# Releasing the next batch's gather at the start of the output projection instead of inside the feed-forward stage

## The chip, the cores and the metric

The kernel runs on one core of one Trainium2 chip. The metric is the device time of one execution in microseconds (us), the median of several runs. The names of the engines are those of the profile: PE is TensorE (PEld its weight loads), DVE is VectorE, ACT is ScalarE, POOL is GpSimd, SP is SyncE. A name with a q (DVEq, POOLq) is the sequencer of that engine, which handles waits and semaphore instructions.

## The reference

Two transformer-like layers over `x` of 4 batches x 1024 tokens x 256 features, float32, each sublayer followed by a residual and a layer norm:

```python
x = ln(x + L0_attn(x))   # a linear state recurrence (scan over the sequence), then a projection
x = ln(x + L0_ffn(x))    # mixture of 8 experts, top 2, each 256 -> 512 -> 256
x = ln(x + L1_attn(x))   # pre-norm softmax attention, 16 heads of 16, projection; it adds its own residual
x = ln(x + L1_ffn(x))    # gated SiLU, 256 -> 704 -> 256, activations and weights quantised to FP4 blocks of 16
```

In the mixture, each token's result is the weighted sum of two experts' results: `out = s0 * y[expert 0] + s1 * y[expert 1]`.

## The kernel before, in words

The kernel has two parts. The first works on all four batches: the scan, the first layer norm, the routing, and then 39 tiles of 256 tokens each through the experts. The expert results are stored in device memory in `y_slot`, in the order of the tiles, and the layer's input is kept in `x_mid`.

The second part is a loop over the four batches, written once and run by every engine as a hardware loop (`Fori(0, B)`). One turn of the loop does, for one batch of 1024 tokens (8 tiles of 128):

1. **Gather (POOL, L457 to L467).** POOL waits for the semaphore flow `qsf`. It then loads the batch's part of `x_mid` (1 MB) into `Xin`, copies the row numbers into `posb` (L461), and issues 16 indirect DMAs (L466), one for each of 8 tiles and each of the two chosen experts, from `y_slot` into `Y1` and `Y2` (128 rows of 1 KB each). `Y1` lies in `Qh`, `Y2` in `Kh`, and `Xin` in the upper half of `V`.
2. **Combine and norm (DVE, L1173 to L1185).** DVE waits for the gather's semaphores, forms `R = Xin + s0*Y1 + s1*Y2` (L1179, L1182), and computes two layer norms.
3. **Attention.** PE turns the tokens, computes Q, K and V, and then for each of 8 head pairs the scores twice (L786 for the row maxima that DVE takes at L1203, L816 for the exponentials that ACT takes at L592) and the weighting of V (L829). POOL sends the maxima as rows (L477), 4 DMAs for each pair.
4. **Output projection.** PE turns the heads' results back (`heads_turn`, L859, flow `op`). DVE divides them by the sums (L1243, L1246). PE turns them again (L881), ACT copies (L601), PE projects (L870, L871), and DVE adds twice the residual (`proj_add`, L1230). This is repeated for 8 tiles.
5. **Norm and quantise (DVE).** The third layer norm (`layer_norm(2, ...)`, L1153 to L1170) and two halves of the FP4 quantiser (L1103 to L1113).
6. **Feed-forward, 8 tiles.** For tile `t`: PE computes gate and up (L903), ACT takes SiLU (L617), DVE multiplies (L1268, flow `hh`) and quantises (L1103 to L1113, flow `hq`), PE turns (L930), ACT copies, PE computes down (L913), and DVE adds the residual (`ffn_add`, L1235).
7. **Last norm and store.** DVE writes `X`, SP stores it.

`qsf` tells POOL that the buffers of the gather are free. Its semaphore is incremented once ahead of the loop (L1139), which releases the gather of the first batch. Inside the loop DVE increments it once in each turn, in the kernel before in tile `t == 1` of the feed-forward stage (L1271, L1272). That increment releases the gather of the next batch; the one of the last turn releases nothing. POOL's queue is in order: it comes to this wait after the last DMA of L477 of the current batch.

All DVE operations that depend on one another are joined by waits on a semaphore (`link`, L1144). An engine's instructions run in the order in which they are written.

Of the kernel before, what the change touches and what calls it, by code (L numbers as in the profile page):

```python
# [78 lines left out]
def transformer(nc, xT, state_cols, WtT, WbT, Wc4, WoT, Dv, bo, sel, Wg, W1, b1, W2, b2, rev,  # L79
                lnw_d, lnb_d, Wqkv, bqkv_d, Wproj, bproj, w_gate, w_up, w_down, ident_d, out):  # L80
    ctx = ExitStack()
    with ctx:
# [853 lines left out]
        def _(dve):  # L936
# [204 lines left out]
            with dve.Fori(0, B) as b:  # L1141
# [91 lines left out]
                def ffn_add(t):  # L1233
                    F["dp"].wait(dve, b, t + 1)
                    F["dr"].inc(dve.tensor_tensor(R2[:, t, :], PS[:, 6 + t % 2, 0:D], X[:, t, :], ALU.add))  # L1235

                for n in range(TT):
                    i, qh = n // 2, n % 2
                    F["op"].wait(dve, b, i + 1)
                    heads = PS[:, 2 * (i % 2):2 * (i % 2) + 2, :].rearrange("p k (h q c) -> p (k h) q c", q=2, c=32)  # L1240
                    if n:
                        F["on"].wait(dve, b, n)
                    link(dve.reciprocal(rc[:, qh, :], heads[:, :, qh, DH]))  # L1243
                    if n >= 2:
                        F["mp"].wait(dve, b, n - 1)
                    F["on"].inc(dve.tensor_tensor(ON[n % 2].rearrange("p (h d) -> p h d", d=DH), heads[:, :, qh, 0:DH],  # L1246
                                                  rc[:, qh, :].unsqueeze(2).to_broadcast([P, HEADS, DH]), ALU.mult))
                    if n >= 2:
                        proj_add(n - 2)
# [16 lines left out]
                for t in range(TT):  # L1266
                    F["sg"].wait(dve, b, t + 1)
                    F["hh"].inc(dve.tensor_tensor(Hb.rearrange("p (a n) -> p a n", a=2), PS[:, 2:4, 0:IH],  # L1268
                                                  SGb.rearrange("p (a n) -> p a n", a=2), ALU.mult))
                    F["hh"].wait(dve, b, t + 1)  # L1270
                    if t == 1:  # L1271
                        dve.sem_inc(F["qsf"].sem, 1)  # L1272
                        F["qsf"].seen += 1
                    for q, ins in enumerate(quant(Hb, P, I, HQ, qn_h, qm_h)):
                        if q < 9:
                            link(ins)
                            if q == 8 and t:
                                F["htp"].wait(dve, b, t)
                        else:
                            F["hq"].inc(ins)  # L1280
                    if t:
                        ffn_add(t - 1)
# [56 lines left out]
```

How the kernel before makes its waits and increments, by code:

```python
    def wait(self, eng, b, n):  # L61
        eng.wait_ge(self.sem, b * self.per + n)
# [12 lines left out]
    def wait(self, eng, n):  # L75
        eng.wait_ge(self.sem, n)
# [240 lines left out]
        @block.sync  # L317
# [75 lines left out]
            load_ffn(1, w_up)  # L393
            load_ffn(2, w_down)
            for k in range(TILES):
                if k + 2 < TILES:
                    load_x(k + 2)
                if k + 1 < TILES:
                    e_next = load_w1(k + 1)
                load_w2(k, e_now)
                e_now = e_next
            sp.wait_ge(s_wev, len(turns))
            sp.wait_ge(s_one, 1)
            for k in range(NB):
                for a in range(2):
# [14 lines left out]
                            for dst, src in ((Qs, qp), (Ks, kp)):  # L421
                                at = ROW * a + row * DH
                                F[f"stk{k}"].inc(sp.dma_start(dst[at:at + DH, k, :].bitcast(F32), src), by=16)
                F["xn"].wait(sp, b, 4 * TT)
                hold(sp, "sp")
                F["outd"].inc(sp.dma_start(out.rearrange("(n p) d -> p n d", p=P)[:, bass.ds(b * TT, TT), :],
                                           X[:, :, :]), by=16)
                F["outd"].wait(sp, b, 16)
                sp.sem_inc(F["xfree"].sem, 1)
                F["xfree"].seen += 1
            sp.wait_ge(F["outd"].sem, 16 * B)
# [51 lines left out]
        @block.scalar  # L483
        def _(act):
            act.preload_act_table_set("natural_log_exp_and_others")
            act.wait_ge(s_const, N_CONST)
            act.wait_ge(s_proT, 2)
            act.wait_ge(s_pro, 2)
```

## Time and profile before

| what | value |
|---|---|
| median of 3 runs | 2095.88 us |
| the 3 runs | 2093.76, 2095.88, 2103.21 us |
| the profiled execution's own time | 2103.21 us |
| its span, first to last instruction | 2101.5 us |
| mean granted TensorE clock over the span | 0.861 of full speed |
| busy share of the span | PE 79%, PEld 45%, DVE 63%, ACT 37%, POOL 11% |

The profile is of one execution. Between the span and the execution's own time lie 1.7 us. Busy shares are means over stages that have different limits, so they don't say what one edit is worth; that is read from the waits and the timeline around it. In a row of waits, the columns are the waiting engine and line, what ended the wait, the total in us, how often, and the longest. In a row of the timeline they are the start in us from the span's start, the duration in us (of all of a merged group), the engine, line, operation, what is written and read, and in square brackets the engine's idle time ahead of it and what ended it.

### The profile page before, as it was taken

Reading aid. Unit: us, or ns where it says so; the run is one execution under the profiler, and the core shown is the slowest. Engines: PE = TensorE matmul, PEld = TensorE weight load, DVE = VectorE, ACT = ScalarE, POOL = GpSimd, SP = SyncE. Lnnn points to the kernel's source line nnn. Section 1 sums busy time; section 2 is a strip of 40 time slices with the busy share of each in tenths; the row PEclk is TensorE's granted clock in tenths of the full one; section 3 lists DMA queues with packets and bytes.
Section 4 is the critical chain, followed back from the end, with each engine's and each line's share of the span. In section 5 each row is a group of like instructions: output and inputs, shape, how many; then the busy total and the mean of one; then the engine's idle time right before and its main releaser. Section 6 shows DMA issues by size and latency. Waiting matters only on the chain.

```text
span 2101.5 us, 26524 instructions
## 1 busy us (share of the span) xinstructions
PE 1656.3 (79%) x7920; PEld 945.7 (45%) x7920; DVE 1333.0 (63%) x2678; ACT 782.2 (37%) x1145; POOL 229.0 (11%) x308
## 2 busy tenths in 40 slices
PE   5751899997389996938999877499996938999686
PEld 2651788886143333624333345243334624333354
DVE  3324223210589956877899287788846877898386
ACT  0220223322127772212676511137671111676421
POOL 0235000002201000300100030000000300001000
PEclk8865899999579997967899988679997967899898
DMA  3223777775131100203120010122000103110000
GB/s 123 73 93 114 247 233 228 228 230 167 34 59 32 32 2 1 61 22 60 18 46 2 1 53 9 42 43 44 17 2 0 61 22 61 29 35 2 1 1 20
DMA packets 90965, 133.77 MB, mean 64 GB/s; under 512 B 17002, under 2 KB 65516, under 8 KB 90812
## 3 DMA queue, kind: packets, MB, share of 16 engines
q1 hardware_dynamic: 76364, 100.15, 18.2%
q0 software_dynamic: 14448, 31.74, 4.5%
q8 instruction: 77, 1.26, 0.3%
q14 instruction: 76, 0.62, 0.1%
HBM read 76.71 MB, written 29.36 MB: 50 GB/s over the span
## 4 chain that ended last, share of the span: by engine, by line
PE 59%; DVE 22%; issue 8%; DMA 3%; ACT 3%; SPq 3%; POOL 1%; another core or an unknown queue 0%; DVEq 0%; ACTq 0%; POOLq 0%
PE PS L786 10%; PE PS L829 10%; DVE MX L1203 9%; PE PS L903 7%; PE PS L710 6%; PE PS L722 6%; PE PS L913 4%; PE PS L816 2%; DVE st L1153 2%; PE PS L764 2%; PE PS L660 2%; PE PS L772 2%; PE PS L870 1%; DVE X L1170 1%; ACT Pb L592 1%
## 5 line engine op out<-in xcount | busy, mean ns | idle before, releaser
L1203 DVE TENSOR_REDUCE MX<-PS 128x1 f32<-128x512 f32 x1024 | 636.4, 682 | 83.5 <-PE PS L786 83.1
L592 ACT ACTIVATE Pb<-PS 128x1024 f32<-128x1024 f32 x512 | 497.8, 1023 | 231.5 <-PE PS L816 230.9
L786 PE MATMUL PS<-Ks,Qs 48*128 48x512 f32 x1024 | 390.6, 494 | 46.5 <-DMA Ks<-OT 19.2
L786 PEld LDWEIGHTS PS<-Ks,Qs 48*128 48x128 f32 x1024 | 175.2, 203 | 365.0 <-DVE MX L1203 326.0
L816 PE MATMUL PS<-Qs,Ks 50*128 50x512 f32 x1024 | 309.7, 453 | 11.8 <-DMA Qs<-MR 5.9
L829 PE MATMUL PS<-Pb,V 128*32 128x512 f32 x2048 | 283.5, 627 | 2.8 <-ACT Pb L592 2.8
L816 PEld LDWEIGHTS PS<-Qs,Ks 50*128 50x128 f32 x1024 | 147.5, 195 | 65.9 <-ACT Pb L592 53.2
L477 POOL DMA_DIRECT2D Qs<-MR x128 | 65.4, 518 | 1024.9 <-DVE MR L1216 597.6
L1135 DVE TENSOR_TENSOR V<-PS,V 128x512 f32<-128x512 f32 x39 | 27.0, 692 | 217.6 <-PE PS L722 217.6
L722 PE MATMUL PS<-Pb,OT 128*128 128x256 f32 x624 | 141.0, 379 | 0.0
L538 ACT ACTIVATE OT<-PS,V 128x256 f32<-128x256 f32 x156 | 65.4, 470 | 159.8 <-PE PS L710 159.8
L753 PE MATMUL PS<-ident,OT 128*128 128x128 f32 x64 | 17.8, 448 | 134.1 <-DVE OT L1170 134.1
L722 PEld LDWEIGHTS PS<-Pb,OT 128*128 128x128 f32 x624 | 115.7, 190 | 14.2
L913 PE MATMUL PS<-wdT,Pb 128*128 128x256 f32 (+1 forms) x384 | 102.5, 412 | 8.0 <-ACT Pb L629 8.0
L903 PE MATMUL PS<-wgT,XT 128*128 128x352 f32 x256 | 92.7, 509 | 16.9 <-DVE OT L1268 8.7
L913 PEld LDWEIGHTS PS<-wdT,Pb 128*128 128x128 f32 (+1 forms) x384 | 74.5, 202 | 35.2 <-issue 10.9
L903 PE MATMUL PS<-wuT,XT 128*128 128x352 f32 x256 | 81.7, 462 | 0.0
L617 ACT ACTIVATE OT<-PS 128x704 f32<-128x704 f32 x32 | 24.2, 757 | 152.7 <-PE PS L903 152.7
L1243 DVE RECIPROCAL rc<-PS 128x16 f32<-128x16 f32 x32 | 8.1, 253 | 107.4 <-PE PS L859 106.6
L710 PE MATMUL PS<-OT,Pb 128*128 128x256 f32 x320 | 75.6, 391 | 0.7 <-ACT OT L529 0.7
L753 PEld LDWEIGHTS PS<-ident,OT 128*128 128x128 f32 x64 | 12.2, 206 | 139.6 <-DVE OT L1170 135.7
L829 PEld LDWEIGHTS PS<-Pb,V 128*32 128x32 f32 x2048 | 40.8, 109 | 74.9 <-issue 65.5
(233 smaller groups left out, 2007.4 us busy)
## 6 DMA issues: line engine op xcount, KB each, us to landing
Pb<-W SPq DMA_DIRECT2D x78, 512.0 KB, 3.9
OT<-x_slot SPq DMA_DIRECT2D x39, 256.0 KB, 4.0
y_slot<-V POOLq DMA_DIRECT2D x39, 256.0 KB, 4.2
Qs<-Qh SPq DMA_DIRECT2D x128, 64.0 KB, 2.3
Ks<-Kh SPq DMA_DIRECT2D x128, 64.0 KB, 2.4
V<-b SPq DMA_DIRECT2D x39, 128.0 KB, 4.3
V<-x_mid POOLq DMA_DIRECT2D x4, 1024.0 KB
out<-X SPq DMA_DIRECT2D x4, 1024.0 KB, 4.6
```

What stands on the lines that cost most here:

```text
L477: F["mrow"].inc(pool.dma_start(Qs[r:r + 1, p % NB, :].rearrange("o (t q) -> o t q", t=TT).bitcast(F32), MR[at:at + TT, p % 2, :].bitcast(F ...
L538: C["hr"].inc(act.activation(HTm[k % 2][:, hc, :], PS[:, 2 + 2 * (k % 2) + hc // 2, hc % 2 * ST:(hc % 2 + 1) * ST], ACT.Relu, bias=b1t[:, ...
L592: F["ex"].inc(act.activation(Pb[:, kt % 2, 2 * qh:2 * qh + 2, :], PS[:, 2 * qh:2 * qh + 2, :], ACT.Exp, scale=0.25))
L660: pe.matmul(o, xTb[b][:, c, t * P:(t + 1) * P], Gm[:, c, :], start=(c == 0), stop=False)
L710: ins = pe.matmul(PS[:, 2 + 2 * (k % 2) + hc // 2, hc % 2 * ST:(hc % 2 + 1) * ST], W1t[k % 2][:, c, hc * P:(hc + 1) * P], XTm[k % 2][:, c, :],
L722: ins = pe.matmul(PS[:, 6 + k % 2, a * D:(a + 1) * D], HTm[k % 2][:, hc, a * P:(a + 1) * P], W2t[k % 2][:, hc, :], start=(hc == 0), stop=( ...
L786: F["slp"].inc(pe.matmul(PS[:, slot_bank(i), :], Qs[rows, p % NB, t * P:(t + 1) * P], Ks[rows, p % NB, kh * HALF:(kh + 1) * HALF], start=T ...
L816: ins = pe.matmul(PS[:, 2 * qh + a, :], Ks[rows, p % NB, kt * P:(kt + 1) * P], Qs[rows, p % NB, qh * HALF:(qh + 1) * HALF], start=True, st ...
L829: ins = pe.matmul(PS[32 * j:32 * j + 32, 7, :], V[:, kt, 2 * p + a, :], Pb[:, kt % 2, 2 * qh + a, :], start=(kt == 0), stop=(kt == KT - 1) ...
L903: ins = pe.matmul(PS[:, 2 * w + a, 0:IH], XT[:, c, t * P:(t + 1) * P], wT[:, c, a * IH:(a + 1) * IH], start=(c == 0), stop=(c == DC - 1))
L913: ins = pe.matmul(PS[:, 6 + t % 2, 0:D], HT[0:k, c, :], wdT[0:k, c, :], start=(c == 0), stop=(c == IC - 1))
L1203: F["sld"].inc(dve.tensor_reduce(MX[:, p % 2, a, t, kh:kh + 1], PS[:, slot_bank(i), :], AX.X, ALU.max))
```

## The change

DVE's increment of `qsf` is taken out of tile 1 of the feed-forward stage and put ahead of the 8 tiles of the output projection. In front of it stands a wait for the first group of turned heads (`op`), the same wait that the first tile's reciprocal has anyway. Nothing else is changed: POOL's instructions and their order, the number of DMAs and their sizes, and the increment ahead of the loop are as before.

```diff
@@ -1234,6 +1234,9 @@
                     F["dp"].wait(dve, b, t + 1)
                     F["dr"].inc(dve.tensor_tensor(R2[:, t, :], PS[:, 6 + t % 2, 0:D], X[:, t, :], ALU.add))
 
+                F["op"].wait(dve, b, 1)
+                dve.sem_inc(F["qsf"].sem, 1)
+                F["qsf"].seen += 1
                 for n in range(TT):
                     i, qh = n // 2, n % 2
                     F["op"].wait(dve, b, i + 1)
@@ -1268,9 +1271,6 @@
                     F["hh"].inc(dve.tensor_tensor(Hb.rearrange("p (a n) -> p a n", a=2), PS[:, 2:4, 0:IH],
                                                   SGb.rearrange("p (a n) -> p a n", a=2), ALU.mult))
                     F["hh"].wait(dve, b, t + 1)
-                    if t == 1:
-                        dve.sem_inc(F["qsf"].sem, 1)
-                        F["qsf"].seen += 1
                     for q, ins in enumerate(quant(Hb, P, I, HQ, qn_h, qm_h)):
                         if q < 9:
                             link(ins)
```

## Rows read from the trace of the kernel before

**Rows 1.** The page, section 4: the chain that ended last, by engine.

```profile
PE 59%; DVE 22%; issue 8%; DMA 3%; ACT 3%; SPq 3%; POOL 1%; another core or an unknown queue 0%; DVEq 0%; ACTq 0%; POOLq 0%
```

**Rows 2.** The waits of all engines over the whole span.

```profile
POOL V L459 <- DVEq L1272: 239.1, 3, 80.2
...
DVE OT L1179 <- DMA Kh<-y_slot,posb: 24.5, 4, 12.2
```

**Rows 3.** The timeline around the first batch's gather, 515 to 560 us.

```profile
517.79 0.91 POOL L459 DMA_DIRECT2D V<-x_mid  x1 [2.68 <-DMA y_slot<-V]
...
526.40 0.88 DVE L1179 SCALAR_TENSOR_TENSOR OT<-Qh,svb,V 128x256 f32<-128x256 f32 x2 [12.22 <-DMA Kh<-y_slot,posb]
...
538.62 0.94 POOL L466 DMA_INDIRECT Kh<-y_slot,posb  x1 [0.30 <-issue]
...
541.36 0.88 DVE L1179 SCALAR_TENSOR_TENSOR OT<-Qh,svb,V 128x256 f32<-128x256 f32 x2 [4.04 <-DMA Kh<-y_slot,posb]
```

**Rows 4.** POOL's timeline, the second batch's gather, first and last instruction.

```profile
851.16 0.93 POOL L459 DMA_DIRECT2D V<-x_mid  x1 [80.19 <-DVEq L1272]
...
873.79 1.46 POOL L466 DMA_INDIRECT Kh<-y_slot,posb  x1 [0.30 <-issue]
```

**Rows 5.** DVE's timeline, where the second batch's combine begins.

```profile
928.10 3.26 DVE L1179 SCALAR_TENSOR_TENSOR OT<-Qh,svb,V 128x256 f32<-128x256 f32 x8 [0.23 <-DVE svb L1173]
```

**Rows 6.** DVE's timeline in feed-forward tiles 0 to 2, first and last loop turn.

```profile
842.87 0.89 DVE L1103 TENSOR_REDUCE qmx<-OT 128x44 f32<-128x704 f32 x1
...
849.41 0.88 DVE L1268 TENSOR_TENSOR OT<-PS,OT 128x704 f32<-128x704 f32 x1
850.45 0.89 DVE L1103 TENSOR_REDUCE qmx<-OT 128x44 f32<-128x704 f32 x1 [0.15 <-DVE OT L1268]
...
858.17 0.42 DVE L1235 TENSOR_TENSOR V<-PS,X 128x256 f32<-128x256 f32 x1 [0.67 <-PE PS L913]
858.51 0.88 DVE L1268 TENSOR_TENSOR OT<-PS,OT 128x704 f32<-128x704 f32 x1
...
2017.87 0.88 DVE L1268 TENSOR_TENSOR OT<-PS,OT 128x704 f32<-128x704 f32 x1
...
2026.98 0.88 DVE L1268 TENSOR_TENSOR OT<-PS,OT 128x704 f32<-128x704 f32 x1
```

**Rows 7.** Windows over tiles 1 to 3: DVE busy (instructions), PEclk, DMA share, GB/s.

```profile
850.40:875.55 25.15, 21.85 (x34) 1.00 0.40 121
...
2018.86:2043.80 24.94, 21.38 (x34) 1.00 0.00 1
```

**Rows 8.** The same two windows, of L1110 alone and of L1111 alone.

```profile
850.40:875.55 25.15, 1.87 (x3) 1.00 0.40 121
2018.86:2043.80 24.94, 1.58 (x3) 1.00 0.00 1
...
850.40:875.55 25.15, 2.67 (x3) 1.00 0.40 121
2018.86:2043.80 24.94, 2.67 (x3) 1.00 0.00 1
```

**Rows 9.** DVE's timeline in the output projection and the norm behind it, first loop turn.

```profile
795.55 0.26 DVE L1243 RECIPROCAL rc<-PS 128x16 f32<-128x16 f32 x1 [27.38 <-PE PS L859]
...
799.27 0.42 DVE L1230 SCALAR_TENSOR_TENSOR V<-X,PS 128x256 f32<-128x256 f32 x1 [1.37 <-PE PS L871]
...
813.85 0.42 DVE L1230 SCALAR_TENSOR_TENSOR V<-X,PS 128x256 f32<-128x256 f32 x1 [1.26 <-PE PS L871]
...
819.60 2.67 DVE L1170 TENSOR_SCALAR X<-V,mv,rstd 128x256 f32<-128x256 f32 x8
822.19 1.21 DVE L1103 TENSOR_REDUCE qmx<-X 128x64 f32<-128x1024 f32 x1
```

**Rows 10.** The chain that ended last in order of time: projection, and two turns' first gate and up.

```profile
797.58 1.03 PE PS L870 x4
...
813.19 0.64 PE PS L871 x2
...
1221.60 8.07 PE PS L903 x16
...
2003.20 6.40 PE PS L903 x16
```

## The prediction

> **What bounds the kernel now.** I read the views in this order. The page's chain by engine comes first: 59% of it is PE, 22% DVE, and 3% DMA [rows 1]. So only a small part of the end is set by transfers, and what I must know is whether the moved gather belongs to that part. The waits answer it. DVE waits for the gather 24.5 us in total, in 4 pieces, the longest 12.2 us [rows 2]. There are four loop turns, so these four pieces could be one in each turn. The timeline shows that they are not: the first is 12.22 us ahead of the combine at 526.40, the last is 4.04 us at 541.36, and the other two lie between them [rows 3]. All four belong to the first batch's gather, which starts at 517.79 right behind the mixture's last store. That gather is released by the increment ahead of the loop, which the change does not touch.
>
> The gathers that the change does move are those of batches 1, 2 and 3. POOL stands idle for them 239.1 us in 3 pieces, each about 80 us, waiting for DVE's increment [rows 2]. The second batch's starts at 851.16 and its last instruction ends at 873.79 + 1.46 = 875.25 [rows 4]. DVE reads its result first at 928.10, and what it waited for then was its own copy of the weights, for 0.23 us, and no transfer [rows 5]. So the gather is finished 928.10 - 875.25 = 52.9 us before it is used, less the landing of its last transfer. For that I take the first batch: the last issue ended at 538.62 + 0.94 = 539.56, and DVE could go on at 541.36 [rows 3], 1.8 us later. About 51 us of slack remain. The other two moved gathers look alike.
>
> **The change part by part.**
>
> (a) *The gather starts earlier.* In the first turn DVE is released by PE at 795.55 [rows 9], the new place of the increment. POOL would start some 0.8 us behind it, as it starts at 851.16 behind the increment that follows the multiply of 849.41 + 0.88 = 850.29 [rows 4, 6]. So it would start near 796.4, about 54.8 us earlier than now. POOL's 80.19 us of idle time [rows 4] show that it is free by 771, so the start really moves. Work hidden before is hidden now with some 106 us of slack instead of 51. Gain: 0. There is no wait there to shorten.
>
> (b) *The gather leaves the feed-forward stage.* Here the trace holds its own comparison. In the last turn there is no gather, and the same 34 DVE instructions of tiles 1 to 3 take 21.38 us busy; with a gather beside them they take 21.85 us [rows 7]. A gather thus stretches DVE's work by 0.47 us, of which L1110, a single-source operation in SBUF, has 1.87 - 1.58 = 0.29 us; L1111, with two SBUF inputs, is the same, 2.67 and 2.67 us [rows 8]. Does DVE's stretch reach the end? From the multiply of tile 1 to that of tile 2 it takes 858.51 - 849.41 = 9.10 us with a gather and 2026.98 - 2017.87 = 9.11 us without, and DVE still waits 0.67 us for PE in between [rows 6]. PE sets the pace and DVE's 0.47 us lies beside it. The removed increment costs 0.15 us of gap in tile 1 against 0.03 us at the same place in tile 0 (842.87 follows directly) [rows 6], also inside that wait. Gain: 0; if DVE were on the path it would be 0.47 + 0.12 = 0.6 us per gather, 3 x 0.6 = 1.8 us. I take 0.
>
> (c) *The gather comes beside the projection and the third norm.* POOL's part lasts from 851.16 to 875.25, 24.1 us, now [rows 4], and 539.56 - 517.79 = 21.8 us where DVE was mostly waiting [rows 3]. From 796.4 it would end between 818.2 and 820.5. Up to 813.85 the chain is PE's, L870 and L871 in turn [rows 10], and DVE waits for PE ahead of its additions, 1.37 us at 799.27 and 1.26 us at 813.85 [rows 9]. So stretches there are hidden. From 813.85 on the chain is DVE's norm. That leaves 820.5 - 813.9 = 6.6 us of overlap on the path. By the price of (b), 0.47 us in 24.1 us, this is 0.13 us. From below it is 0, because the single-source operations of the norm come at its end, from 819.60 on [rows 9], when POOL has nearly finished. From above it is all 0.47 us. I take 0.13 us, for 3 gathers 0.4 us. Nothing reaches the quantiser from 822.19 on, which has the kind of operation that was stretched.
>
> The rule that speaks against this move is in the Trainium skill, "GPSIMD Engine Reference", section "Key points": GpSimd shares its SBUF interfaces with VectorE, and they contend where a VectorE instruction runs in a 2-port mode or has two SBUF inputs. The trace agrees on L1110 and shows nothing on DVE's side for L1111, 2.67 us either way [rows 8]. The Trainium skill, "VectorE: DVE Perf Modes", section "Why PSUM operands drop a tier", says that an operand in PSUM excludes the 2-port mode, so the projection's DVE work, which all reads PSUM, would be exposed less; by that the sum would be 0.4 us smaller at most.
>
> (d) *The increment on DVE ahead of the first reciprocal.* It is on the chain: PE's turned heads release DVE at 795.55 [rows 9], and the increment stands between. Behind it in DVE's queue are all of the projection's operations, for which PE waits. The nearest row is the gap of (b), 0.15 - 0.03 = 0.12 us; from below it is 0, if the sequencer takes it within its own latency. The added wait is for the same value as the next one, and costs no more than that. I take 0.12 us in each of the 4 turns, 0.5 us.
>
> (e) *Other queues.* SP issues nothing between the attention's stacks and the last store, and POOL's next work behind the gather is the next batch's maxima, over 100 us later. ACT has no operation added. The DMA engines are 0.40 busy during a gather and 0.00 without one [rows 7], with PE at the same pace.
>
> Sum: 0 + 0 + 0.4 + 0.5 = +0.9 us. Against the profiled execution's 2103.21 us this gives 2104.1. That execution is the slowest of the three runs, and the change touches nothing that made it so; carried to the median of 2095.88 the sum gives 2096.8, which I round to **2097 us**.
>
> **The rivals.** A measurement of this kernel can tell about 0.5%, 10.5 us, from no change; that is 3.5 us for each of the three moved gathers.
>
> *Rival 1, slower: POOL's issuing stalls DVE and PE in the projection.* The projection passes each tile from PE to DVE to PE to ACT and back, and a stall in any link could add up. The largest single delay that I would price is the 0.29 us of L1110 over three tiles [rows 8], charged once to each of POOL's 17 DMA instructions: 17 x 0.29 = 4.9 us per gather, 14.8 us in all, with the increment 2111 us. It decides from 0.2 us per POOL instruction. Against it: the whole of 34 DVE instructions lost only 0.47 us beside a gather [rows 7], and PE's pace did not change.
>
> *Rival 2, faster: the feed-forward stage is relieved.* If DVE's stretch were on the path, 1.8 us come back, and 2094 us results, still no measurable change. For over 10.5 us a gather would have to hold up that stage by 3.5 us now. The 9.10 and 9.11 us [rows 6] exclude that for tile 1 to 2, and only something outside those tiles could give it; 2085 us would be its time.
>
> *Rival 3: the clock moves.* The same 16 matmuls at the head of the feed-forward stage take 8.07 us in one turn and 6.40 us in another [rows 10], in one execution. A small shift of when PE rests can change such pieces: 3 x 1.67 = 5.0 us to either side, 2092 to 2102 us. That stays within 0.5% and would look like the spread of the three runs, 9.45 us.
>
> *Rival 4: the change doesn't do what it says*, that is, POOL starts no earlier. POOL's idle 80 us exclude it but for a cause that I don't see; the time would be 2096 us.
>
> **How the numbers follow.** The forecast (0.9 us more, with the clock's movement of rival 3 about it) has 0.82, rival 4 has 0.02. Rival 1 has 0.09, rival 2's large form 0.05, and its small form 0.02. So within 0.5% have 0.82 + 0.02 + 0.02 = 0.86; slower 0.09; faster 0.05. The range: low is 2095.88 - 1.8 (all of rival 2's small form) - 5.0 (clock) = 2089. High is the slowest of the runs shown, 2103.21, plus the upper ends 3 x 0.47 + 4 x 0.12 = 1.9 us, which is 2105, and one more for part of rival 1: 2106.
>
> **What would show each step.** In the changed kernel's trace the gathers of batches 1 to 3 start about 0.8 us behind the first turned heads and end near the norm's last operations. DVE's wait for the gather is still about 24.5 us in 4 pieces, all in the first batch. Feed-forward tiles keep their 9.1 us, and the 34 instructions of tiles 1 to 3 fall from 21.85 to 21.38 us in the first three turns. From 795.55 to 822.19, 26.6 us, the same stretch grows by 0.1 to 0.6 us in the first three turns and by about 0.1 us in the last. The prediction is wrong if that stretch grows by over 3 us, or if a feed-forward tile of the first three turns comes under 9.0 us.

## The result and the profile after

The changed kernel takes 2147.3 us (median of 4 runs, 2145.53 to 2149.53), the kernel before 2096.76 us (4 runs, 2093.76 to 2103.21). The ratio is 1.0238, 95% interval 1.0211 to 1.0264. It is slower by 50.5 us, far outside the range that was forecast (2089 to 2106 us). The profiled execution took 2139.71 us with a span of 2138.0 us, 36.5 us over the profiled span of before.

The page of the changed kernel, section 4, the chain by engine, answers to [rows 1]:

```profile
PE 58%; DVE 21%; issue 9%; ACT 3%; SPq 2%; DMA 2%; another core or an unknown queue 2%; POOL 1%; DVEq 0%; ACTq 0%; POOLq 0%
```

"Another core or an unknown queue" rose from 0% to 2%. The kernel has one core, so this is time that ended with an event for which the profile has no sender.

The waits of the changed kernel, as in [rows 2], and DVE's multiplies of feed-forward tiles 1 and 2, as in [rows 6]:

```profile
POOL V L459 <- DVEq L1238: 71.5, 3, 24.6
...
DVE OT L1179 <- DMA Kh<-y_slot,posb: 24.5, 4, 12.2
```

```profile
857.09 0.88 DVE L1271 TENSOR_TENSOR OT<-PS,OT 128x704 f32<-128x704 f32 x1
...
866.19 0.88 DVE L1271 TENSOR_TENSOR OT<-PS,OT 128x704 f32<-128x704 f32 x1
```

The moved gathers are released early (24.6 us of idle POOL time in place of 80), DVE's wait for gathers is the same to a tenth, and a feed-forward tile still takes 866.19 - 857.09 = 9.10 us.

The first and the last loop turn of the changed kernel, from the first reciprocal to the quantiser, DVE's timeline, as in [rows 9]:

```profile
788.36 0.26 DVE L1246 RECIPROCAL rc<-PS 128x16 f32<-128x16 f32 x1 [25.50 <-PE PS L859]
...
804.50 0.42 DVE L1230 SCALAR_TENSOR_TENSOR V<-X,PS 128x256 f32<-128x256 f32 x1 [6.80 <-PE PS L871]
...
805.13 0.42 DVE L1249 TENSOR_TENSOR Pb<-PS,rc 128x256 f32<-128x256 f32 x1
813.61 0.42 DVE L1230 SCALAR_TENSOR_TENSOR V<-X,PS 128x256 f32<-128x256 f32 x1 [8.06 <-remote]
...
829.79 1.21 DVE L1103 TENSOR_REDUCE qmx<-X 128x64 f32<-128x1024 f32 x1
...
2000.30 0.26 DVE L1246 RECIPROCAL rc<-PS 128x16 f32<-128x16 f32 x1 [26.63 <-PE PS L859]
...
2026.93 1.21 DVE L1103 TENSOR_REDUCE qmx<-X 128x64 f32<-128x1024 f32 x1
```

In the first turn this stretch takes 829.79 - 788.36 = 41.43 us, in the last, which has no gather, 2026.93 - 2000.30 = 26.63 us. All four turns: 41.43, 41.43, 40.70, 26.63; before, 26.64 in each. That is 14.8, 14.8 and 14.1 us more (14.6 on average), together 43.6 us. The rest of the span balances: the first reciprocal came 7.2 us earlier in this execution (788.36 against 795.55 in [rows 9]), the pieces between and behind the four stretches differ by -3.0 to +1.4 us and add up to 0.1 us, and 43.6 - 7.2 + 0.1 = 36.5 us, the difference of the spans. So the whole loss of the profiled execution sits in this stretch, in the three turns that have a gather. The medians are further apart, 36.5 + 6.5 + 7.6 = 50.6 us, because the profiled execution of before lies 6.5 us above its median and that of the changed kernel 7.6 us below its own. So 44 of the 50.5 us are found, and about 7 us are in executions that were not profiled.

What happens in this stretch, in the first turn: POOL's timeline (first and last indirect DMA), then PE's and ACT's:

```profile
791.04 1.04 POOL L466 DMA_INDIRECT Qh<-y_slot,posb  x1 [0.84 <-POOL posb L461]
...
809.93 0.95 POOL L466 DMA_INDIRECT Kh<-y_slot,posb  x1 [0.30 <-issue]
```

```profile
798.66 0.69 PE L871 MATMUL PS<-bproj_sb,ones_row 1*128 1x256 f32 x2
...
802.01 1.20 PE L871 MATMUL PS<-bproj_sb,ones_row 1*128 1x256 f32 x2
805.61 0.69 PE L881 MATMUL PS<-ident,Pb 128*128 128x128 f32 x2 [2.40 <-DVE Pb L1249]
...
818.19 2.08 PE L870 MATMUL PS<-wproj,XT 128*128 128x256 f32 x4
```

```profile
800.27 0.62 ACT L601 ACTIVATE XT<-PS,bqkv 128x128 f32<-128x128 f32 x2 [4.48 <-issue]
807.32 0.62 ACT L601 ACTIVATE XT<-PS,bqkv 128x128 f32<-128x128 f32 x2 [6.42 <-PE PS L881]
813.65 0.62 ACT L601 ACTIVATE XT<-PS,bqkv 128x128 f32<-128x128 f32 x2 [5.72 <-remote]
```

The reader is to see three things. The fourth tile's L871 is recorded as over at 798.66 + 0.69 = 799.35, and DVE, whose addition waits for just that, starts at 804.50, 5.2 us later. The fifth's is over at 802.01 + 1.20 = 803.21, and its addition starts at 813.61, 10.4 us later. Where no gather runs, DVE waits 1.3 us in all for these matmuls [rows 9]. The other direction is prompt: DVE's product ends at 805.13 + 0.42 = 805.55, and PE, which waits for it, starts at 805.61. And everything that waits for PE goes on at the same moment, DVE at 813.61 and ACT at 813.65, 2.7 us behind the end of POOL's last indirect DMA instruction (809.93 + 0.95 = 810.88). ACT's copies wait in the same way: the one at 807.32 is for turned heads that were recorded as over at 799.28 + 0.44 = 799.72. So in this turn what PE hands over comes late while POOL issues indirect DMAs, and what DVE hands to PE does not.

The windows of the changed kernel over the same stretch (length, busy PE, PEld, DVE, ACT, POOL, then PEclk, DMA share, GB/s):

```profile
785.00:800.00 15.00, 13.25 (x76) 8.64 (x76) 5.08 (x15) 3.36 (x10) 7.96 (x10) 1.00 0.39 123
800.00:815.00 15.00, 6.46 (x16) 3.41 (x17) 2.35 (x7) 1.87 (x6) 8.44 (x9) 0.57 0.30 87
815.00:830.00 15.00, 6.41 (x14) 3.38 (x13) 7.94 (x32) 1.04 (x4) 0.00 (x0) 0.50 0.00 1
```

The granted clock goes from 2.4 to 1.2 GHz early in the stall, not at its end. PE rests from 799.72 to 800.95, 1.2 us, and the fifth tile's L871, from 802.01, already takes 1.20 us for 2 instructions, where the tile before took 0.69. It stays at 1.2 GHz to the end of the stretch: the last tile's L870 takes 2.08 us for 4 instructions at 818.19, where before it took 1.03 [rows 10]. So part of the 14.8 us is the clock's. A lower bound of that part is what comes behind the last late hand-over. The last four additions take 821.45 - 813.61 = 7.84 us from the first to the last of them; before they took 813.85 - 808.45 = 5.40 us, with the clock at full. That is 2.4 us. From DVE's timelines, the kernel before and the changed one (the last addition of before is in [rows 9]):

```profile
808.45 0.42 DVE L1230 SCALAR_TENSOR_TENSOR V<-X,PS 128x256 f32<-128x256 f32 x1 [0.81 <-PE PS L871]
```

```profile
821.45 0.42 DVE L1230 SCALAR_TENSOR_TENSOR V<-X,PS 128x256 f32<-128x256 f32 x1 [2.73 <-PE PS L871]
```

### The profile page after: what moved, and what is told of

It is laid out like the page before. It is cut to its first block, busy times and chain, and to the rows that moved or that the text cites. A ratio compares the mean times of both kernels' runs of the same rounds, so it can differ in the third digit from the quotient of the medians.

```text
span 2138.0 us, 26524 instructions
## 1 busy us (share of the span) xinstructions
PE 1668.1 (78%) x7920; PEld 952.5 (45%) x7920; DVE 1330.9 (62%) x2678; ACT 781.9 (37%) x1145; POOL 222.0 (10%) x308
## 3 DMA queue, kind: packets, MB, share of 16 engines
q8 instruction: 77, 1.26, 0.2%
## 4 chain that ended last, share of the span: by engine, by line
PE 58%; DVE 21%; issue 9%; ACT 3%; SPq 2%; DMA 2%; another core or an unknown queue 2%; POOL 1%; DVEq 0%; ACTq 0%; POOLq 0%
PE PS L786 10%; PE PS L829 9%; DVE MX L1203 9%; PE PS L903 7%; PE PS L710 6%; PE PS L722 6%; PE PS L913 4%; PE PS L816 2%; DVE st L1153 2%; PE PS L764 2%; PE PS L772 2%; PE PS L660 2%; PE PS L870 1%; DVE X L1170 1%
## 5 line engine op out<-in xcount | busy, mean ns | idle before, releaser
L816 PE MATMUL PS<-Qs,Ks 50*128 50x512 f32 x1024 | 307.7, 450 | 13.1 <-DMA Qs<-MR 6.7
```

Source lines behind the costliest of these rows:

```text
L816: ins = pe.matmul(PS[:, 2 * qh + a, :], Ks[rows, p % NB, kt * P:(kt + 1) * P], Qs[rows, p % NB, qh * HALF:(qh + 1) * HALF], start=True, st ...
```

## The experiments

**1. Is it the early release, or what runs beside it?** Two kernels put the release or the transfers elsewhere.

```diff
# e1_norm: kernel before, DVE's increment moved behind the last addition of the projection
+                dve.sem_inc(F["qsf"].sem, 1)
+                F["qsf"].seen += 1
                 layer_norm(2, R2, X, None)
```

> The gather of the next batch is released behind the last addition of the output projection, ahead of the third norm, so it runs beside the norm, the quantiser and the first feed-forward tile. Theory: beside the gather PE's semaphore increments arrive late, and this costs time only where PE hands over many short steps, as in the projection; here 2097 us (2089 to 2106), the stretch from the first reciprocal of the projection to the quantiser 26.6 us again, and no PE increment is late. Rival: any early release costs, because the gather disturbs whatever chain it lies beside; then the norm and the quantiser (some 30 us of DVE work on the path) grow by several us in each of three turns and the time is above 2110 us.

```diff
# e2_xin_only: changed kernel, only the 1 MB load is early; the indirect DMAs wait for a second flow
+                F["qsg"].wait(pool, b, 1)          # behind the load; DVE increments it in feed-forward tile 1
```

> Only the 1 MB load of x_mid is released at the projection; the 16 indirect DMAs of each gather stay in feed-forward tile 1, behind a second semaphore. Theory (the many small gather DMAs with their completions are what delays PE's increments): 2097 us, the projection's stretch 26.6 us. Rival (the traffic as such, or POOL's being active in that stage): the 1 MB moves in about 4 us at the highest rate of the whole gather, so at least a quarter of the 14.8 us per turn stays, 2107 us or more.

In the session of these two, of e3_pool_direct and of e4_dense_ffn, the kernel before took 2105.32 us (26 runs). Released ahead of the norm: 2103.07 us, ratio 0.9989 [0.9970, 1.0009], stretch 26.8 us in all turns, though its gather runs from 821.35 to 844.45, beside the norm and the quantiser. Only the load early: 2101.73 us, ratio 0.9982 [0.9969, 0.9995], stretch 26.6 us. So the norm and the quantiser don't suffer, and the load alone does no harm. Of the places tried so far, only the projection is hurt, and it takes the indirect DMAs.

**2. Is it the indirect form?**

```diff
# e3_pool_direct: changed kernel, direct DMAs of the same 128 rows of 1 KB
-                        F[f"gat{t // 2}"].inc(pool.indirect_dma_start(dst[:, t, :], None, y_slot[:, :],
-                            bass.IndirectOffsetOnAxis(posb[:, k, t:t + 1], 0)), by=16)
+                        F[f"gat{t // 2}"].inc(pool.dma_start(
+                            dst[:, t, :], y_slot[(2 * t + k) * P:(2 * t + k + 1) * P, :]), by=16)
```

It leaves out the choice of rows by the routing.

> Release at the projection as in the changed kernel, but the 16 indirect DMAs are direct ones of the same 128 rows of 1 KB from fixed rows (the selection of rows by the routing is left out, in all four batches). Theory A (the indirect form matters): the projection's stretch goes back to 26.6 us and the time to about 2097 us. Theory B (any stream of 16 DMAs issued by POOL delays PE's increments): the stretch stays near 41 us. POOL may issue them faster, about 0.93 us each as for the x_mid load, so under B a little less than 41 us.

2092.49 us (3 runs), ratio 0.9943 [0.9916, 0.9970], stretch 26.6 us in all turns. (The time is below that of before because the first batch's gather, which is on the path, is shorter in this form: DVE waits 14.0 us for it in place of 24.5.) POOL issues the same bytes at the same place in 9.3 us (794.20 + 0.54 - 785.49), in place of 19.8, and nothing is held up. The hold-back was there in that execution: its routing waits (experiment 7) are 12.38 and 12.59 us. From POOL's timeline:

```profile
785.49 0.56 POOL L466 DMA_DIRECT2D Qh<-y_slot  x1 [0.62 <-POOL posb L461]
...
794.20 0.54 POOL L466 DMA_DIRECT2D Kh<-y_slot  x1
```

That they are over sooner does not explain it: 8 indirect DMAs, issued in 9.8 us, do hold the projection up (e8_half, experiment 5).

**3. Is it bytes, or PE's number of signals?** Three kernels varied these.

```diff
# e6_narrow: changed kernel, each indirect DMA moves 64 of the 256 columns (a quarter of the data);
# with two memsets ahead of the loop, not shown
+                            dst[:, t, 0:64], None, y_slot.rearrange("r (q d) -> (r q) d", q=4),
+                            bass.IndirectOffsetOnAxis(posb[:, k, t:t + 1], 0)), by=16)
# e9_dense_proj: changed kernel, a spare increment on every matmul of the projection that had none,
# one of three places shown
+                        if p < NP - 1:
+                            ins.then_inc(spare["pe"], 1)
# e4_dense_ffn: kernel before, the same on the matmuls of gate, up and down; one of two places shown
+                        if c < IC - 1:
+                            ins.then_inc(spare["pe"], 1)
```

> The changed kernel with indirect DMAs that move 64 of 256 columns of each row (from a narrower view, so other rows; three quarters of each row are left out), with two memsets of some 4 us ahead of the loop. Theory A (POOL's making of the indirect descriptors delays PE's increments): the stretch stays near 41 us in the first three turns. Theory B (the bytes or the writes into SBUF matter): it falls by the share of the bytes, to under 31 us.

> The changed kernel with a further increment, for which nobody waits, on each matmul of the projection that has none: 14 increments a tile more or less in place of 3. Theory A (PE's increments wait in a queue that is served slowly while indirect DMAs are issued): the queue is longer, the first three turns' stretch rises clearly over 41.4 us, towards 50 us and more. Theory B (each handover is late by itself, or PE itself is held, whatever the number of increments): 41 us within 1.5 us. The fourth turn 26.6 us either way.

> The kernel before, in which every matmul of gate, up and down also increments a semaphore that nobody waits for: PE then posts about one increment every 0.3 us in the feed-forward stage instead of three in 9.1 us. Theory (what the gather delays is a queue of PE's increments, so the rate decides): tiles 1 to 3 of the first three turns, which run beside the gather, take over 9.5 us each and the last turn's 9.1 us; 2105 us or more. Rival (something special to the projection, such as its one-row bias matmul or its instructions' place): 9.1 us in all four turns, 2097 us.

A quarter of the bytes: stretch 41.66, 41.68, 41.60 and 26.64 us, 2146.74 us (2 runs; before 2102.94 in its session), ratio 1.0206 [1.0158, 1.0254]. More increments: 41.48, 41.51, 41.45, 26.65 us, 2143.26 us (2 runs; before 2097.17 in its session), ratio 1.0213 [1.0148, 1.0279]. So neither bytes nor a queue of PE's increments makes the size of it. The number of rows for each DMA, 128, was the same in all runs and is not tested. In the feed-forward stage of the kernel before, dense increments beside the gather lengthened one tile interval in each of the three turns with a gather, to 9.35, 9.42 and 9.28 us in place of 9.10, and none in the last turn. That is 0.2 to 0.3 us for a gather. The kernel stayed at 2102.96 us, ratio 0.9996 [0.9981, 1.0011]. My theory, that the rate of signals sets how much a stage suffers, fell with these runs; a small effect of it in the feed-forward stage is there.

**4. Is it the projection's one-row bias matmul, and does PE's own work matter?**

```diff
# e5_no_bias_row: changed kernel without the matmul of L871 (the bias is left out)
# e10_busy_proj: changed kernel, 4 unread matmuls ahead of each L870 and of each L881 group
+                    for _ in range(4):
+                        pe.matmul(PS[:, 6 + n % 2, D:2 * D], ident[:, :], wproj[:, 0, :], start=True, stop=True)
```

> The changed kernel without the projection's one-row bias matmuls (the output projection's bias is left out); PE posts as many increments as before. Theory A (PE's increments of whatever instruction are late while the indirect DMAs of the gather are issued): the stretch from the projection's first reciprocal to the quantiser keeps some 15 us over its undisturbed length (which falls from 26.6 us to about 21.5 us, 8 x 0.62 us less), so 34 to 38 us in the first three turns. Theory B (the one-row matmul is what the gather holds up): the first three turns are as short as the fourth.

> The changed kernel with 8 more matmuls in each of the 8 projection tiles, whose results nobody reads, so that PE hardly rests. The fourth turn, without a gather, gives the undisturbed length, about 26.6 + 8 x 1.8 = 41 us at most. Theory A (increments are late only where PE rests between handovers, which would be why the feed-forward stage is spared): the first three turns are within 1 us of the fourth. Theory B (the rest of PE has nothing to do with it): they are 8 us or more longer.

Without the bias the stretch is 36.59, 36.66, 36.66 us and 20.94 us in the turn without a gather: 15.7 us more, so that matmul is not the cause (2127.42 us, 2 runs, ratio 1.0114 [1.0065, 1.0164]). With PE kept busy, 60.28, 61.05, 59.30 against 53.75 us: 5.6 to 7.3 us more in place of 14.8 (the kernel takes 2230.55 us, 2 runs, ratio 1.0629 [1.0562, 1.0697], because of the added matmuls). It came out between what the theories expected, and decides nothing between them. It does show that the projection loses less when PE has more work in it. Two causes are mixed in that. The late hand-overs can be covered by the added work. And the clock hardly falls: its mean over the three long stretches is 0.89 to 0.94, against 0.97 in the last, where the changed kernel's goes from 0.86 to 0.67. The feed-forward stage, where 16 matmuls stand behind each wait, fits either, but neither was shown to be the reason why it is spared.

**5. Is it general, and does it grow with the number?**

```diff
# e7_attn: kernel before, 8 indirect DMAs into a scratch tile in the fourth head pair of each turn
# (the loop over t and the last wait are not shown)
+                            F["scr"].inc(pool.indirect_dma_start(
+                                scr[:, t, :], None, y_slot[:, :], bass.IndirectOffsetOnAxis(posb[:, 0, t:t + 1], 0)), by=16)
# e8_half: changed kernel, the last 8 of the 16 indirect DMAs wait until feed-forward tile 1
+                    if t == TT // 2:
+                        F["qsg"].wait(pool, b, 1)
```

> The kernel before with 8 further indirect DMAs of 128 rows into a scratch buffer in each turn, issued by POOL in the attention of the fourth head pair, where PE, DVE and ACT hand over every 0.5 us. Theory A (it is general: any stage of dense handovers from PE is stalled by indirect DMAs): a head pair takes 22.3 us now and the one with the DMAs 5 us or more longer, in all four turns; 2120 us or more. Theory B (special to the projection): 22.3 us and 2100 us, within 5 us.

> The changed kernel, but only x_mid and the first 8 indirect DMAs are released at the projection, the other 8 in feed-forward tile 1. In the changed kernel the long waits began only behind the sixth indirect DMA. Theory A (the delays build up with the DMAs issued and end with them): the 8th ends some 12 us behind the release, so 3 to 8 us of the 14.8 us stay, the stretch 30 to 35 us. Theory B (each DMA costs the same): half, 34 us. Rival (the stall needs no POOL activity at all): 41 us.

In the attention a head pair takes 22.3 us. DVE's timeline of e7_attn, the end of two pairs' maxima, with the first and last scratch DMA between them:

```profile
675.49 0.19 DVE L1215 TENSOR_REDUCE NM<-MX 128x16 f32<-128x32 f32 x1
...
693.88 2.48 DVE L1211 TENSOR_REDUCE MX<-PS 128x1 f32<-128x512 f32 x4 [6.85 <-remote]
...
707.83 0.19 DVE L1215 TENSOR_REDUCE NM<-MX 128x16 f32<-128x32 f32 x1
```

```profile
681.58 1.02 POOL L485 DMA_INDIRECT scr<-y_slot,posb  x1 [0.30 <-issue]
...
690.48 0.95 POOL L485 DMA_INDIRECT scr<-y_slot,posb  x1 [0.30 <-issue]
```

707.83 - 675.49 = 32.34 us, 10 us more; 32.65, 32.28 and 32.28 in the other turns. The kernel took 2141.45 us (2 runs), ratio 1.0181 [1.0103, 1.0259]. So it is not special to the projection. Here too the clock falls: 0.57 from 690 to 695, and 0.50 from 695 to 700.

Half of the gather early: 35.07, 33.80, 33.82 us, which is 7.2 to 8.4 us more; 2122.34 us (3 runs), ratio 1.0110 [1.0055, 1.0165]. That is about half of the loss, but it is not one cost for each DMA. DVE's timeline of e8_half, the fourth and the last addition of the first turn, whose first reciprocal is at 794.87, and the fourth addition of the kernel before:

```profile
809.05 0.42 DVE L1234 SCALAR_TENSOR_TENSOR V<-X,PS 128x256 f32<-128x256 f32 x1 [4.82 <-remote]
...
821.60 0.42 DVE L1234 SCALAR_TENSOR_TENSOR V<-X,PS 128x256 f32<-128x256 f32 x1 [2.73 <-PE PS L874]
```

```profile
806.60 0.42 DVE L1230 SCALAR_TENSOR_TENSOR V<-X,PS 128x256 f32<-128x256 f32 x1 [1.68 <-PE PS L871]
```

The fourth addition comes 14.18 us behind the first reciprocal, in the kernel before 806.60 - 795.55 = 11.05 us: 3.1 us late. From there to the last it takes 12.55 us in place of 813.85 - 806.60 = 7.25 us, another 5.3 us. No indirect DMA is issued then (the eighth was over at 807.40), and PE is busy for 12.57 us of the 13.1 us from 809.00 to 822.10, with the clock at 0.50. So the larger part of the 8.4 us is the low clock that the stall left behind. In the other two turns it is 3.1 us late and 4.1 us by the clock.

**6. Does it take DMAs that pile up?**

```diff
# e11_paced: changed kernel, each indirect DMA waits until the one ahead has landed
+                        if t or k:
+                            F[f"gat{j // 4}"].wait(pool, b, 16 * (j % 4 + 1))     # j = 2 * t + k - 1
```

> The changed kernel, in which POOL issues each indirect DMA of a gather only when the one before has landed, about 3 us each, so a gather takes some 50 us in place of 21; the first batch's becomes longer too, by about 30 us, on the path. Theory A (DMAs piling up on POOL's queue cause the delay): the first three turns' projection stretch is 26.6 us again, and the time 2096 + 30 = some 2125 us. Theory B (each making of descriptors holds PE's increments back for a while): some of the stall stays, 30 us or more.

```profile
826.41 0.26 DVE L1250 RECIPROCAL rc<-PS 128x16 f32<-128x16 f32 x1 [25.48 <-PE PS L863]
...
853.05 1.21 DVE L1107 TENSOR_REDUCE qmx<-X 128x64 f32<-128x1024 f32 x1
```

```profile
829.10 1.04 POOL L470 DMA_INDIRECT Qh<-y_slot,posb  x1 [0.85 <-POOL posb L461]
834.24 0.98 POOL L470 DMA_INDIRECT Kh<-y_slot,posb  x1 [4.09 <-DMA Qh<-y_slot,posb]
```

DVE's and POOL's timelines of this kernel: 853.05 - 826.41 = 26.64 us with the early release in place and the gather beside the projection; 26.72, 26.67 and 26.65 in the other turns. One indirect DMA at a time holds nothing back, though in the same execution the unpaced scatters of the routing stage do (11.38 and 11.94 us, experiment 7). So neither the place nor the indirect form alone is the cause; it takes indirect DMAs that don't wait for one another, 1.25 us apart (0.95 + 0.30) in the changed kernel. One thing weakens this run. The paced DMAs start 3.5 to 5.1 us apart, so only six of the sixteen fall into the stretch, and in the changed kernel, too, no wait of DVE was longer until the sixth had been issued, at 797.43. A stall that needs more than six in a row, at whatever pace, is excluded here only by what stands in experiment 7. The kernel is still slow, 2137.33 us (2 runs), ratio 1.0185 [1.0112, 1.0258], because the first gather, which is on the path, was paced too: the first reciprocal comes at 826.41, some 31 us late.

**7. It was in the kernel before all along.** The routing stage scatters with the same form of DMA (L443). From the trace of the kernel before, DVE's timeline, then POOL's:

```profile
75.20 0.17 DVE L990 TENSOR_TENSOR yt<-y 128x8 f32<-128x8 f32 x1 [1.59 <-ACT y L500]
...
110.51 0.17 DVE L990 TENSOR_TENSOR yt<-y 128x8 f32<-128x8 f32 x1 [12.05 <-ACT y L500]
...
148.19 0.17 DVE L990 TENSOR_TENSOR yt<-y 128x8 f32<-128x8 f32 x1 [11.95 <-ACT y L500]
```

```profile
86.96 1.15 POOL L443 DMA_INDIRECT x_slot<-X,pos  x1 [85.14 <-DVE pos L1032]
...
106.13 0.96 POOL L443 DMA_INDIRECT x_slot<-X,pos  x1 [0.30 <-issue]
124.67 0.95 POOL L443 DMA_INDIRECT x_slot<-Qh,pos  x1 [17.58 <-DVE pos L1032]
...
143.63 0.96 POOL L443 DMA_INDIRECT x_slot<-Qh,pos  x1 [0.30 <-issue]
```

The same operation waits 1.59 us where no scatter runs and 12 us where 16 of them do, twice, and ends 3.4 to 3.6 us behind POOL's last one. If that is the same effect, pacing the scatters must gain.

```diff
# e12_scatter2 and e16_scatter2_again: kernel before, two chains of semaphores, so that at most two scatters
# of batches 0 and 1 are in flight (the waits of SP and ACT for the two chains are not shown)
+                        if b < 2 and t:
+                            C[f"sca{b % 2}{k}"].wait(pool, 16 * t)
```

> The kernel before with the indirect scatters of the routing stage (line 443, batches 0 and 1) paced so that at most two are in flight; nothing else changed. Theory A (indirect DMAs issued back to back hold back what waits for TensorE): the two waits of the routing chain on ACT's logits of about 12.0 us each shrink to about 1.6 us, which they take where no scatter is issued, and the kernel gains what the chain does not hide, 10 to 21 us: 2076 to 2087 us where the kernel before takes 2097. Theory B (the 12 us waits of the routing chain are its own work, and the late signals are only of the gathers beside the projection): the waits stay at 12 us, and the time is that of before or up to 10 us more through the slower scatters.

The runs of this study were made in seven sessions, each with its own runs of the kernel before. The first try at this one, with two other kernels, fell in a session of another kind. The kernel before took 2068.77 us there (25 runs, 2060.74 to 2074.86), 28 us and more below all earlier sessions, and e12_scatter2 2067.74 us, ratio 1.0001 [0.9984, 1.0018]. The unpaced scatters of e14_attn_direct, profiled in that session, show the routing wait at 1.59, 1.59 and 1.56 us: nothing was held back there at all. This is also the control for the reading above, since the same unpaced scatters run beside the same chain. So nothing could be gained. The two kernels sent with it were

> The changed kernel with its gather paced so that at most two indirect DMAs are in flight (the run with one in flight at a time took 2137 us, with no stall of the projection and a first gather some 31 us longer on the path). Theory A with a threshold above two: the stretch from the first reciprocal to the quantiser stays at 26.6 us in all four turns, the first gather is 10 to 18 us shorter than with one in flight, and the time is 2095 to 2125 us. Theory A with a threshold below two: the stretch is between 28 and 41 us in the three turns with a gather.

> The run with eight indirect DMAs beside an attention pair, with direct DMAs of POOL of the same rows and sizes in their place. Theory A (it is the indirect form): the pair takes 22.3 us again in place of 32.3, and the kernel the time of before within 6 us. Rival (any eight transfers issued by POOL beside TensorE-paced work do it): the pair stays at 30 us or more and the time at about 2140 us.

and they had 26.6 to 27.0 us in the stretch (2079.39 us, ratio 1.0051 [1.0030, 1.0073]) and 22.3 us in the head pair (2068.53 us, ratio 1.0000 [0.9984, 1.0016]). In such a session that tells nothing of the pacing or of the form. One view differs between the two kinds of session, the landings of the DMA issues (KB each, median us from issue to landing, where the profile finds it). First e14_attn_direct, then the kernel before:

```profile
x_slot<-X,pos POOLq DMA_INDIRECT x32, 2.4
...
Qh<-y_slot,posb POOLq DMA_INDIRECT x32, 2.8
```

```profile
x_slot<-X,pos POOLq DMA_INDIRECT x32
...
Qh<-y_slot,posb POOLq DMA_INDIRECT x32
```

Where PE's hand-overs are late, the profile finds no landing of the unpaced indirect DMAs; where they are not late, it finds the unpaced gathers at 2.7 to 2.8 us. (In e11_paced, in the first kind of session, the paced gathers have 2.8 us and the unpaced scatters none.) The row of the gathers is the one to read. That of the scatters misleads: in the last session below, without a hold-back, `x_slot<-X,pos` has no landing either. The surer sign is the routing wait itself. The question was put again in another session.

> The changed kernel once more, unaltered, because the last three runs were measured on a chip on which the kernel before takes 2069 us and on which the two 12 us waits of its routing stage are only 1.6 us although the scatters are issued back to back there. Theory C (the hold-back is there on some chips and not on others): on a chip whose routing stage shows waits of 1.6 us, the stretch from the first reciprocal to the quantiser is 26.6 us in all four turns and the changed kernel is within 0.5% of the kernel before; on a chip whose routing stage shows waits of about 12 us, the stretch is 41 us in three turns and the changed kernel 2.0 to 2.6% slower. Rival (the two signatures have different causes): the routing waits are 1.6 us and the stretch is still 41 us, or the other way round.

> The kernel before with its scatters paced two in flight, once more. Theory A with C: on a chip whose routing stage shows waits of about 12 us with unpaced scatters, these waits fall to about 1.6 us and the kernel is 15 to 28 us faster than the kernel before; on the other kind of chip it is the same within 0.5%, as in the first run. If two in flight do not suffice, the waits stay above 5 us and the gain is under 10 us.

There the hold-back was found: before 2096.79 us (13 runs), the changed kernel 2141.51 us, ratio 1.0207 [1.0162, 1.0253], with 40.72, 41.44, 40.70 and 26.63 us in the stretch and 11.59 and 12.03 us in the routing waits. The chip was the one of the session before, so it is no fixed trait of a chip. And e16_scatter2_again gained: 2087.77 us (10 runs), ratio 0.9947 [0.9921, 0.9972], 9 us. DVE's timeline of it, then POOL's:

```profile
74.21 0.17 DVE L994 TENSOR_TENSOR yt<-y 128x8 f32<-128x8 f32 x1 [1.59 <-ACT y L503]
...
101.41 0.17 DVE L994 TENSOR_TENSOR yt<-y 128x8 f32<-128x8 f32 x1 [4.23 <-ACT lnv L501]
...
134.55 0.17 DVE L994 TENSOR_TENSOR yt<-y 128x8 f32<-128x8 f32 x1 [6.84 <-ACT y L503]
```

```profile
86.22 1.15 POOL L446 DMA_INDIRECT x_slot<-X,pos  x1 [84.40 <-DVE pos L1036]
...
106.33 0.96 POOL L446 DMA_INDIRECT x_slot<-X,pos  x1 [0.32 <-issue]
```

The waits fell from 12 to 4.2 and 6.8 us and not to 1.6, and the gain is below the 15 to 28 us that I expected. Two in flight hold back less than sixteen issued without a wait, but still some. And the pace of issue is nearly the same: from the first to the sixteenth scatter of the first batch it takes 106.33 - 86.22 = 20.1 us, in the kernel before 106.13 - 86.96 = 19.2 us. So all sixteen are there, 1.34 us apart in place of 1.28, and the waits fall by 5 to 8 us. How close together they are issued and how many there are in a row does not explain that. What this run and e11_paced share is that each indirect DMA waits for one ahead of it to land. The kernel is faster than both the one before, by 0.5%, and the changed one.

**8. The last two** repeated the open kernels, and fell again in a session without the hold-back (before 2069.98 us, 19 runs; routing waits 1.59 us in both).

> The changed kernel with its gather paced two in flight, once more (its first run fell in a session without the hold-back: routing waits of 1.6 us beside unpaced scatters). If the routing waits are about 12 us in this run too, the session tells: with one indirect DMA in flight there was no stall (26.6 us), and with scatters two in flight the routing waits were 4 to 7 us in place of 12. Theory A (the hold-back grows with the number in flight): the stretch from the first reciprocal to the quantiser is 28 to 36 us in the three turns with a gather, and the time 2105 to 2130 us. Rival (reads are held back only by more than two in flight): the stretch is 26.6 to 27.0 us and the time 2100 to 2115 us, about 0.5% above before as in the first run.

> The attention run with direct DMAs in the place of the eight indirect ones, once more, for the same reason. Theory A (it is the indirect form), in a session with routing waits of about 12 us: the head pair takes 22.3 us, as without any of them, where the indirect ones made it 32.3, and the kernel is the same as before within 0.5%. Rival (any eight transfers issued by POOL beside TensorE-paced work do it): the pair takes 30 us or more and the kernel about 2140 us.

Gather two in flight: 26.6 to 26.7 us, 2077.80 us, ratio 1.0032 [1.0007, 1.0056]. Direct DMAs in the attention: 22.3 us, 2065.07 us, ratio 0.9982 [0.9962, 1.0002]. Neither decides what it was sent for.

## Why the prediction was wrong, by its steps

**(a) and (b) held.** The gathers start 0.7 us behind the first reciprocal, DVE's wait for gathers is still 24.5 us in 4 pieces, feed-forward tiles keep 9.10 us, and the 34 DVE instructions of tiles 1 to 3 fall from 21.85 to 21.29 us in the first turn: there was nothing to gain, as said. (e) is true of what it names, but its last argument, the DMA engines busy "with PE at the same pace", was read in the feed-forward stage and does not hold in the projection.

**(d) held, size and all.** The increment stands ahead of the first reciprocal, so it must be looked for there and not in the stretch, as the prediction's list of signs had it. From PE's first turned heads (L859) to the reciprocal it takes 788.36 - 787.10 = 1.26 us in the first turn, before 795.55 - 794.42 = 1.13 us, and the same in the other turns within 0.01 us: 0.13 us where 0.12 was said. The two rows of PE, changed kernel and kernel before:

```profile
787.10 1.97 PE L859 MATMUL PS<-ident,OT 128*128 128x128 f32 x16 [0.72 <-ACT OT L551]
```

```profile
794.42 1.97 PE L859 MATMUL PS<-ident,OT 128*128 128x128 f32 x16 [0.72 <-ACT OT L551]
```

**(c) is the step that failed.** It said that stretches beside the projection "are hidden" and put 0.13 us per gather, 0.47 us at most. It measured 14.6 us on average. The price came from one resource, DVE's busy time in the feed-forward stage, and was carried to a stage where another thing is scarce. The projection passes each tile PE, DVE, PE, ACT, PE, DVE, and each step waits for the signal of the one ahead. What got worse first is no operation's duration but how late PE's hand-over is seen; PE's own durations grew only with the fall of the clock that followed. [rows 7] count busy time and can't show that.

**Rival 1 had the direction and not the size or the mechanism.** It asked for a stall in the chain of engines, but by 0.29 us per POOL instruction, for 4.9 us per gather. By its own count of 17 instructions 14.6 us is 0.86 us each. Its argument against itself, that PE's pace in the feed-forward stage did not change, is true and was the wrong witness. Its price, DVE's largest single delay, was taken from the stage that is spared. The right witness was in the same trace: wait times of one line with and without indirect DMAs beside it (experiment 7), 12 us per 16 of them in place of 1.6. With those rows an estimate would have been about 10 us per gather, 30 us in all, without the clock.

**The clock (rival 3)** was priced by itself, at 1.67 us per turn. It came as a consequence: PE idled, and the clock went to half. It took at least 2.4 us of the first turn's 14.8 us, and 5.3 of 8.4 us in e8_half.

Shown: indirect DMAs issued without waiting for one another lengthen the projection (the changed kernel against e3_pool_direct, and against e11_paced with the weakness named there), a head pair of the attention (e7_attn) and the routing (e16_scatter2_again), not by their bytes (e6_narrow), and not in every session; and the low clock that follows makes part of the loss (e8_half). Open: whether the matmuls themselves end late or only their signals, since the ends of matmuls are modelled in the profile; why a DMA that waits for another's landing does no or less harm at nearly the same pace; why the feed-forward stage is nearly spared (e10_busy_proj only hints); whether direct DMAs are harmless in the attention too, since both runs of that fell in sessions without the hold-back; what makes a session one of the two kinds; whether the changed kernel is slower in a session without the hold-back, since it never ran in one (the paced one lost 0.3 to 0.5% there, with nothing in this stretch, and pacing lengthens its first gather); and how many in flight the projection bears, since one did no harm and eight issued without a wait did; the scatters show some with two.

## What to carry to other kernels

Before a burst of indirect DMAs is moved, ask what runs beside it in the new place, and whether that work is a chain of short hand-overs from PE or long blocks that wait for nobody. Price it from the same trace, by the waits of one line with and without such DMAs beside it, not by busy times. Where a burst must lie beside such a chain, letting its DMAs wait for one another's landing helped. With one in flight the stall was gone (the gather), but the transfer is longer, so that belongs only where it is not on the path. With two (the scatters) more than half of it was gone, at under 1 us more for 16 DMAs.

## What the runs showed of the hardware that I had not expected

While indirect DMAs were issued 1.25 us apart without waiting for one another, what waited for PE went on up to 10.4 us late, and the last of it 2.7 us after the last of them was issued; hand-overs to PE were prompt (0.06 us).
